# Third layer of a four-layer graph network: VectorE fills destination rows 40 columns ahead of the running sums instead of 48

## The chip, the core and the metric

The kernel runs on one core of one Trainium2 chip. The metric is the device time of the whole program in microseconds (us): the median of several executions. The rows shown come from one further execution, which the hardware profiler recorded.

## The reference

Four layers of message passing over one graph, each followed by a residual and a layer norm. The graph has 6250 nodes of 64 features and 106250 edges, sorted by destination. The third layer, the only one that the change touches, is an attention layer with six heads:

```python
def _L2_gnn_ref(x, edge_idx, W_l, W_r, att, bias):      # the third layer
    ...
    gl = (x @ W_l).reshape(n, H, F_OUT)                   # H = 6, F_OUT = 64
    gr = (x @ W_r).reshape(n, H, F_OUT)
    s = jax.nn.leaky_relu(gl[src] + gr[dst], NEG_SLOPE)
    e = jnp.einsum('ehf,hf->eh', s, att)                  # a logit for each edge and head
    m = jax.ops.segment_max(e, dst, num_segments=n)
    p = jnp.exp(e - m[dst])
    denom = jax.ops.segment_sum(p, dst, num_segments=n)
    alpha = p / (denom[dst] + 1e-16)
    msg = alpha[:, :, None] * gl[src]
    out = jax.ops.segment_sum(msg, dst, num_segments=n)
    out = out.mean(axis=1) + bias
    return jax.nn.selu(out)
...
x = _layernorm(x + _L0_gnn_ref(...)); x = _layernorm(x + _L1_gnn_ref(...))
x = _layernorm(x + _L2_gnn_ref(x, edge_index, ...));  x = _layernorm(x + _L3_gnn_ref(...))
```

## The kernel before

The edges stand as a table of 128 partitions by NC = 832 columns, so that a column holds 128 edges, one for each partition, and each partition walks through 832 edges in the order of their destinations. The third layer goes through the columns in NCH = 52 chunks of CH = 16. Five queues work on it, all written out by hand, with semaphores between them. Instructions of one queue start in the order in which they stand.

**GpSimd (POOL), `g2_chunk`.** One indirect DMA for each column gathers the 128 rows of the source nodes (table `xt2`, both halves of 64 values alike) into the tile XS, which holds NX = 6 chunks. A gather into a column that was used six chunks ago waits for the sums of that column. The issuing line is the helper L193. The landings of eight columns are counted together: a semaphore for each half chunk.

**VectorE (DVE).** It has four kinds of work for each chunk c.
- `fill2(c, j)`, L1355: the second half of a gathered row is to be the destination's row. Where the edge has the same destination as the edge of the column before, the row is copied from there (a predicated copy of 64 values); else the gathered one stays. So the fills of all 832 columns are one chain, and each half chunk waits for its gathers to land (j = 0 and j = 8).
- `soft2(c, 0..5)`, L1466 to L1480: running maxima of the logits over a chunk, in six small instructions.
- `px2` (L1514), the products of the source rows with the first four heads' weights, two columns at a time, and `carry2` (L1502).
- `step2(c, j)`, L1548 for j = 0 and L1550 for the rest: the running sum of 390 values over the columns. Here it is "the sum" of column j.

In the loop the order for each j is: a fill of a column further on, for j = 8, 9 and 10 two instructions of `soft2(c + 1)` around the sum, the sum, and after each even j a `px2`. The next chunk begins with `carry2`.

**TensorE (PE).** `chunk2_t(c)` takes a chunk in four quarters of four columns: `pt_t` transposes four columns (L1367), `pm_t` multiplies the quarter before by the weights in three pieces (L1382), and at the second quarter `pe_t` and `pf_t` (L1398, L1411) make the logits of chunk c - 1. Before quarters 0 and 2 it waits for the fill of column 7 and of column 15.

**ScalarE (ACT).** `exp2_a(c + 1)` (L1489, L1490, L1495) needs all of `soft2(c + 1)`. Behind it in the queue come 18 items of chunk c + 3 from A_ORDER, mixed with 33 items of `px2_a(c + 1)` (L1528, then L1533: the products for the last two heads, from which each pair of sums waits). Items 0, 4, 8 and 12 are the copies of the transposed quarters (`pt_a`, L1374), three items behind each are `pm_a` (L1389), and items 16 and 17, which stand behind item 7, copy the logits of chunk c + 2 (`pe_a` L1406, `pf_a` L1416):

```python
for n, i in enumerate(A_ORDER):      # 0..7, 16, 17, 8..15
    if c + 3 < NCH:
        chunk2_a(e, c + 3, i)
    ...
    while at * 18 < (n + 1) * 33:
        px2_a(e, c + 1, at)
        at += 1
```

The items of `px2_a` are numbered from 0 (L1528) to 32. Before the sum of an even column j the product item 2j + 4 must be done: item 4 for j = 0, item 16 for j = 6, item 20 for j = 8, item 32 for j = 14.

**SyncE** stores the sums of a chunk (3.2 MB) once its last sum is done.

Of the kernel before, what the change touches and what calls it, by code (L numbers as in the profile page):

```python
# [12 lines left out]
NC = 832  # L13
EP = P * NC
CH = 16
NCH = NC // CH
# [44 lines left out]
def gathered_before(L, b):  # L61

    late = sum(16 * CH // 2 for n in (N0, N1)[0:L] if b == (NCH - 1) % n)
    return sum(16 * CH // h * len(range(b // h, NCH, n)) for n, h in ((N0, 1), (N1, 1), (NX, 2), (4, 1))[0:L] if b // h < n) - late
# [8 lines left out]
def bc(a, shape):  # L76
    return a.broadcast_to(shape)
# [6 lines left out]
def build(nc, x, src, dst, et16, et8, w0, beta, wl, wr, att, bias2, w3, coeff, hbias, loopw, out):  # L84
# [22 lines left out]
    with ExitStack() as ctx:  # L107
# [12 lines left out]
        S = {n: ctx.enter_context(nc.semaphore("k_" + n)) for n in names}  # L120
# [1186 lines left out]
        def xsv(c):  # L1307
            return XS[:, c % NX, :].rearrange("p (j d) -> p j d", j=CH)
# [7 lines left out]
        def q2_at(c):  # L1316
            return 6 * c - 2 if c else 0

        def f2_at(c, j):

            if c < 4:
                return 16 * c + j + 1
            return 64 + 9 * (c - 4) + (9 if j == 15 else (j + 1) // 2 + (j == 14))

        def g2_chunk(e, c, general):
            for j in range(CH):
# [15 lines left out]
        def fill2(e, c, j):  # L1342
            cur, prv = xsv(c), xsv(c - 1)
            if j % 8 == 0:
                k = 2 * (c % NX) + j // 8
                e.wait_ge(S[f"g_{k}"], gathered_before(2, k) + 8 * CH * (c // NX + 1))
            if c == 0 and j == 0:
                e.wait_ge(S["xdi"], 32)
                v.tensor_copy(cur[:, 0, D:P], xi2[:, 0:D]).then_inc(S["f2"], 1)
                return  # L1350
            if c >= 4 and j % 2 and j < CH - 1:
                e.wait_ge(S["t2"], 16 * (c - 3) + j - 1)
            else:
                e.wait_ge(S["f2"], f2_at(c, j - 1) if j else f2_at(c - 1, CH - 1))
            m = v.copy_predicated(cur[:, j, D:P], bc(gi[:, c * CH + j:c * CH + j + 1], [P, D]),  # L1355
                                  cur[:, j - 1, D:P] if j else prv[:, CH - 1, D:P])
            if c < 4 or j % 2 or j == CH - 2:
                m.then_inc(S["f2"], 1)

        def pt_t(e, u):  # L1360
            c, q = divmod(u, NGR)
            if q % 2 == 0:
                e.wait_ge(S["f2"], f2_at(c, 4 * q + 7))
            if u >= 2:
                e.wait_ge(S["at"], u - 1)
            for i in range(4):
                m = t.transpose(PS[u % 2][:, i * P:(i + 1) * P], xsv(c)[:, 4 * q + i, :], ident[:])  # L1367
            m.then_inc(S["pt"], 1)
# [83 lines left out]
        def soft2(e, c, i):  # L1452

            Sp = s2v(c - 1)
            pq = pf2[:, c % 2, H * CH:H * CH + H]
            if c == 0 and i in (1, 5):
                return
            n = q2_at(c) + (i - 1 if c == 0 and i else i)
            if n:
                e.wait_ge(S["q2"], n)  # L1460
            if i == 0:
                e.wait_ge(S["ab"], c + 1)
                e.wait_ge(S["init"], 17)
                if c:
                    e.wait_ge(S["am"], c)
                m = v.tensor_copy(Bf[:, :, 1:CH], bc(Bn[:, c * CH + 1:(c + 1) * CH].unsqueeze(1), [P, H, CH - 1]))  # L1466
            elif i == 1:
                m = v.scalar_tensor_tensor(out=eb[:, :, 0], in0=Sp[:, CH - 1, HW:], scalar=Bn[:, c * CH:c * CH + 1],
                                           in1=eb[:, :, 0], op0=ALU.add, op1=ALU.max)
            elif i == 2:  # L1470
                m = v.tensor_tensor_scan(mf2.rearrange("p h j -> p (h j)"), Bf.rearrange("p h j -> p (h j)"),  # L1471
                                         eb.rearrange("p h j -> p (h j)"), -BIG, ALU.add, ALU.max)
            elif i == 3:
                m = v.tensor_tensor_scan(mb2.rearrange("p h j -> p (h j)")[:, ::-1], Bb[:, 1:][:, ::-1],  # L1474
                                         mf2.rearrange("p h j -> p (h j)")[:, ::-1], -BIG, ALU.add, ALU.max)
            elif i == 4:
                m = v.tensor_tensor(p2v(c).rearrange("p h (q i) -> p h q i", q=4), logits,
                                    mb2.rearrange("p h (q i) -> p h q i", q=4), ALU.subtract)
            else:
                m = v.scalar_tensor_tensor(out=pq, in0=Sp[:, CH - 1, HW:], scalar=Bn[:, c * CH:c * CH + 1],  # L1480
                                           in1=mb2[:, :, 0], op0=ALU.add, op1=ALU.subtract)
            m.then_inc(S["q2"], 1)
# [14 lines left out]
        def carry2(e, c):  # L1497

            pq = pw2[c % 2][:, H * CH:H * CH + H]
            e.wait_ge(S["ax"], c + 1)  # L1500
            e.wait_ge(S["t2"], 16 * c - 1)
            v.tensor_tensor(tmp2, s2v(c - 1)[:, CH - 1, 0:HW].rearrange("p (h d) -> p h d", h=H),  # L1502
                            bc(pq.unsqueeze(2), [P, H, 65]), ALU.mult)

        def px2(e, c, k):

            n = HV
            cols = slice(2 * k, 2 * k + 2)
            pe_ = pw2[c % 2][:, 0:H * CH].rearrange("p (h j) -> p j h", h=H)
            if k == 0:  # L1510
                e.wait_ge(S["ax"], c + 1)
                if c >= 2:
                    e.wait_ge(S[f"s_{c % 2}"], stored_before(2, c % 2) + 16 * (c // 2))
            m = v.tensor_tensor(s2v(c)[:, cols, 0:n * 65].rearrange("p j (h d) -> p j h d", h=n)[:, :, :, 0:D],  # L1514
                            bc(xsv(c)[:, cols, 0:D].unsqueeze(2), [P, 2, n, D]),
                            bc(pe_[:, cols, 0:n].unsqueeze(3), [P, 2, n, D]), ALU.mult)
            if k == 0:
                m.then_inc(S["p2"], 1)
# [18 lines left out]
        def step2(e, c, j):  # L1537
            if c == 0 and j == 0:
                return
            Sv = s2v(c)  # L1540
            if j == 0 or (c == 0 and j == 1):
                e.wait_ge(S["p2"], c + 1)
            if j % 2 == 0 or (c == 0 and j == 1):
                e.wait_ge(S["ap"], 8 * c + j // 2 + 1)
            if c or j > 1:
                e.wait_ge(S["t2"], 16 * c + j - 1)
            if j == 0:
                m = v.tensor_tensor(Sv[:, 0, 0:HW], Sv[:, 0, 0:HW], tmp2.rearrange("p h d -> p (h d)"), ALU.add)  # L1548
            else:
                m = v.scalar_tensor_tensor(out=Sv[:, j, 0:HW], in0=Sv[:, j - 1, 0:HW],  # L1550
                                           scalar=gf[:, c * CH + j:c * CH + j + 1], in1=Sv[:, j, 0:HW],
                                           op0=ALU.mult, op1=ALU.add)
            m.then_inc(S["t2"], 1)

        def layer2_v(e):
            vc.hold()
            v.memset(Bb, -BIG).then_inc(S["init"], 1)
            for c in range(2):
                for j in range(CH):
                    fill2(e, c, j)  # L1560
            for i in range(6):
                soft2(e, 0, i)
            for j in range(CH):
                fill2(e, 2, j)
            for c in range(NCH):
                if c:
                    carry2(e, c)
                px2(e, c, 0)
                for j in range(CH):
                    if c + 3 < NCH:  # L1570
                        fill2(e, c + 3, j)
                    if c + 1 < NCH and 8 <= j < 11:
                        soft2(e, c + 1, 2 * j - 16)
                    step2(e, c, j)
                    if c + 1 < NCH and 8 <= j < 11:
                        soft2(e, c + 1, 2 * j - 15)
                    if j % 2 == 0 and j + 2 < CH:
                        px2(e, c, j // 2 + 1)
                    if c == NCH - 1 and j < 13:
                        if j == 0:  # L1580
                            e.wait_ge(S["am"], NCH)
                        mend_max_v(e, vc, 2, T2, H, B2, j)
# [706 lines left out]
        def _(e):  # L2289
# [128 lines left out]
            with e.If(oneway2 != 0):  # L2418
                e.wait_ge(S["xt"], 64 * NG)
                exchange_v(e, 2)  # L2420
            layer2_v(e)
            mend_soft_v(e, vc, 2, T2, H, B2)
            e.wait_ge(S["fr"], 1)
# [135 lines left out]
```

## Time and profile before

| what | value |
|---|---|
| median of 3 runs | 4737.09 us (4735.63 to 4739.78) |
| profiled execution: time | 4745.29 us |
| profiled execution: span | 4743.1 us |
| third layer's column loop | from about 2335 to 3464 us of the span |
| busy over the whole span | POOL 72%, DVE 58%, ACT 35%, PE 31% |
| busy tenths in the slices of the loop | DVE 8, ACT 8, PE 8, POOL 7 |

The span runs from the first to the last instruction; the time of the profiled execution is 2.2 us longer, and 8.2 us above the median. In the rows below, a row of the timeline gives start, duration, engine, line and operation, how many instructions are merged, and in brackets how long the engine sat idle before it and what ended that. A row of the windows gives, for each engine, busy time and count of instructions, then TensorE's granted clock as a share of full speed, the DMA engines' busy share and GB/s.

### The profile page before, as it was taken

To read this page: it belongs to the slowest core of one execution; us is meant where nothing else is said; L and a number is where in the kernel's file an instruction comes from. 1 tells how busy PE (TensorE), PEld (TensorE's weight loads), DVE (VectorE), ACT (ScalarE), POOL (GpSimd) and SP (SyncE) were. 2 spreads that over 40 slices of the span, in tenths; PEclk is the share of its full clock that TensorE was granted. 3 is DMA by queue.
4 is the path that set the end of the run, shared out by engine and by line. 5 is a ranking of instruction groups with operands and counts; after the bars stand their busy time and mean duration, and the time that the engine had idled before them with its cause. 6 is when DMAs were issued, how large, how long until landed. Compare 5 with 4: busy or idle time off the path is not lost.

```text
span 4743.1 us, 28267 instructions
## 1 busy us (share of the span) xinstructions
PE 1448.4 (31%) x6129; PEld 722.0 (15%) x6129; DVE 2738.1 (58%) x5205; ACT 1643.2 (35%) x3774; POOL 3421.7 (72%) x3538
## 2 busy tenths in 40 slices
PE   7721111000000000001788888888832000000003
PEld 3610000000000000000333333333332000000002
DVE  4684443116555555556378888888875444444444
ACT  2232212220011111112378888888842222221121
POOL 6777777776777777776577777777454777777776
PEclk9955555555555555555899999999965555555555
DMA  7222222223233333332245555555541222222222
GB/s 279 51 75 52 50 50 53 53 55 56 71 80 80 80 80 80 80 81 73 50 161 216 204 201 216 214 197 209 198 140 48 79 80 79 79 72 78 79 79 75
DMA packets 183555, 502.21 MB, mean 106 GB/s; under 512 B 91670, under 2 KB 94044, under 8 KB 167112
## 3 DMA queue, kind: packets, MB, share of 16 engines
q0 software_dynamic: 114560, 181.19, 17.4%
q1 hardware_dynamic: 66584, 316.93, 17.4%
q10 hardware_dynamic: 2224, 2.13, 0.2%
q8 instruction: 53, 0.87, 0.1%
q14 instruction: 134, 1.10, 0.1%
HBM read 185.63 MB, written 314.17 MB: 105 GB/s over the span
## 4 chain that ended last, share of the span: by engine, by line
POOL 29%; issue 10%; DVE 6%; DMA 4%; PE 2%; ACT 1%; POOLq 0%; DVEq 0%; SPq 0%; ACTq 0%
POOL AR L193 29%; DMA AR<-xt,Si 3%; DVE AR L1550 2%; DVE AR L1514 1%; PE ps L1242 0%; PE ps L1398 0%; PE ps L1719 0%; PE ps L1382 0%; DVE AR L1355 0%; ACT AR L1389 0%; ACT AR L1533 0%; DVE AR L1474 0%; DVE AR L1471 0%; ACT AR L1707 0%; PE ps L1726 0%
## 5 line engine op out<-in xcount | busy, mean ns | idle before, releaser
L193 POOL DMA_INDIRECT AR<-xt,Si x2496 | 2399.5, 961 | 807.3 <-issue 732.4
L193 POOL DMA_INDIRECT AR<-y,R x752 | 721.1, 959 | 234.8 <-issue 227.6
L1382 PE MATMUL ps<-AR,WLR 128*128 128x512 f32 x1248 | 612.9, 614 | 94.4 <-ACT AR L1389 94.4
L1865 DVE TENSOR_TENSOR AR<-AR,ps 128x2048 f32<-128x2048 f32 (+1 forms) x53 | 186.7, 3522 | 561.4 <-DMA AR<-xt,Si 561.4
L1533 ACT ACTIVATE AR<-AR 128x64 f32<-128x64 f32 x1664 | 498.5, 349 | 0.0
L1550 DVE SCALAR_TENSOR_TENSOR AR<-AR,gf 128x390 f32<-128x390 f32 x780 | 482.7, 619 | 5.7 <-ACT AR L1533 3.2
L1824 ACT COPY AR<-AR 128x2048 f32<-128x2048 f32 (+1 forms) x53 | 189.1, 3568 | 837.4 <-DVE AR L1883 837.4
L1389 ACT ACTIVATE AR<-ps 128x512 f32<-128x512 f32 x624 | 370.8, 594 | 70.0 <-PE ps L1382 68.6
L890 DVE SCALAR_TENSOR_TENSOR AR<-ps,AR 128x1024 f32<-128x1024 f32 x52 | 102.6, 1973 | 439.8 <-DMA AR<-xt,Si 439.8
L1174 PE MATMUL ps<-AR,ones 128*128 128x384 f32 (+1 forms) x6 | 3.7, 758 | 1072.2 <-DVE AR L1125 1072.2
L946 ACT ACTIVATE ps<-AR 128x17 f32<-128x17 f32 (+1 forms) x52 | 9.8, 188 | 911.4 <-DVE AR L930 884.1
L543 DVE SCALAR_TENSOR_TENSOR AR<-AR,gf 128x64 f32<-128x64 f32 x48 | 15.8, 328 | 490.7 <-ACT AR L527 490.7
L1355 DVE COPY_PREDICATED AR<-gf,AR 128x64 f32<-128x64 int32 x831 | 187.8, 226 | 188.7 <-DMA AR<-xt,Si 187.3
L193 POOL DMA_INDIRECT AR<-s,endi x196 | 219.3, 1119 | 95.5 <-issue 66.1
L1514 DVE TENSOR_TENSOR AR<-AR,ps 128x512 f32<-128x512 f32 x416 | 282.7, 680 | 0.0
L1382 PEld LDWEIGHTS ps<-AR,WLR 128*128 128x128 f32 x1248 | 215.0, 192 | 350.6 <-issue 258.3
L1914 PE MATMUL ps<-LW,AR 128*128 128x64 f32 (+1 forms) x98 | 24.1, 428 | 773.8 <-ACT AR L1906 773.8
L527 ACT COPY AR<-AR 128x1024 f32<-128x1024 f32 (+1 forms) x48 | 90.6, 1888 | 440.0 <-DMA AR<-y,R 440.0
L1883 DVE TENSOR_TENSOR_SCAN AR<-ps,AR 128x512 f32<-128x512 f32 x208 | 241.6, 1200 | 0.0
L375 PE MATMUL ps<-AR 128*128 128x196 bf16 x416 | 77.4, 367 | 514.3 <-DVE AR L368 514.3
L1398 PE MATMUL ps<-AR,A 128*32 128x512 f32 x1248 | 206.2, 628 | 0.0
L1174 PEld LDWEIGHTS ps<-AR,ones 128*128 128x128 f32 x6 | 1.7, 320 | 1073.2 <-DVE AR L1125 1072.6
(345 smaller groups left out, 3496.0 us busy)
## 6 DMA issues: line engine op xcount, KB each, us to landing
s<-AR SPq DMA_DIRECT2D x51, 3168.0 KB
s<-AR SPq DMA_DIRECT2D x51, 1024.0 KB, 4.0
AR<-xt,Si POOLq DMA_INDIRECT x2496, 2.5
s<-AR SPq DMA_DIRECT2D x53, 512.0 KB, 2.7
s<-AR SPq DMA_DIRECT2D x51, 528.0 KB, 3.0
y<-AR SPq DMA_DIRECT2D x24, 1024.0 KB, 4.1
AR<-y,R POOLq DMA_INDIRECT x752, 2.4
xt<-X SPq DMA_DIRECT2D x21, 224.0 KB, 3.1
```

Source lines behind the costliest of these rows:

```text
L193: g.indirect_dma_start(out=o, out_offset=None, in_=table, in_offset=bass.IndirectOffsetOnAxis(ap=idx, axis=0)).then_inc(S[sem], 16)
L890: m = v.scalar_tensor_tensor(out=tx1(c), in0=bc(gx1(c)[:, 0:CH].unsqueeze(1), [P, D, CH]), scalar=0.5, in1=g1v(c)[:, :, 65:R1].rearrange(" ...
L1355: m = v.copy_predicated(cur[:, j, D:P], bc(gi[:, c * CH + j:c * CH + j + 1], [P, D]), cur[:, j - 1, D:P] if j else prv[:, CH - 1, D:P])
L1382: t.matmul(PS[2 + k % 3][:], WLR[:, ch * P:(ch + 1) * P], XT2[:, u % 6, :], start=True, stop=True).then_inc(S["pm"], 1)
L1389: s.activation(RL2[:, u % 5, ch * 512:(ch + 1) * 512], PS[2 + k % 3][:], ACT.Relu).then_inc(S["ar"], 1)
L1398: m = t.matmul(PS[6][32 * q:32 * q + 32, :], w_, m_, start=(ch == 0), stop=(ch == 3))
L1514: m = v.tensor_tensor(s2v(c)[:, cols, 0:n * 65].rearrange("p j (h d) -> p j h d", h=n)[:, :, :, 0:D], bc(xsv(c)[:, cols, 0:D].unsqueeze(2) ...
L1533: m = s.activation(Sv[:, j, h * 65:h * 65 + D], xsv(c)[:, j, 0:D], ACT.Copy, scale=pe_[:, h, j:j + 1])
L1550: m = v.scalar_tensor_tensor(out=Sv[:, j, 0:HW], in0=Sv[:, j - 1, 0:HW], scalar=gf[:, c * CH + j:c * CH + j + 1], in1=Sv[:, j, 0:HW], op0= ...
L1824: s.copy(s3v(c)[:, j0:j0 + n, :], sum3(i).rearrange("p x j -> p j x")).then_inc(S["co"], 1)
L1865: v.tensor_tensor(sum3(i).rearrange("p (b d) j -> p j b d", b=NBS), bc(rows.unsqueeze(2), [P, n, NBS, D]), bc(CW3[:, i % 2, :, 0:n].rearra ...
L1883: v.tensor_tensor_scan(part, gx3(i)[:], part, 0.0, ALU.mult, ALU.add).then_inc(S["sc"], 1)
```

## The change

The number of columns that VectorE's fills run ahead of its sums becomes a constant, AHEAD = 40. Before, 48 columns (three chunks) were filled ahead of the loop, and at column j of chunk c the fill was that of column j of chunk c + 3. Now 40 are filled ahead, and at column 16c + j the fill is that of column 16c + j + 40: for j = 0 to 7 columns 8 to 15 of chunk c + 2, for j = 8 to 15 columns 0 to 7 of chunk c + 3. The semaphore counts follow.

```diff
+        AHEAD = 40
+
         def f2_at(c, j):
 
-            if c < 4:
-                return 16 * c + j + 1
-            return 64 + 9 * (c - 4) + (9 if j == 15 else (j + 1) // 2 + (j == 14))
+            at = CH * c + j
+            if at < AHEAD + CH:
+                return at + 1
+            k, i = divmod(at - AHEAD - CH, CH)
+            return AHEAD + CH + 9 * k + (9 if i == CH - 1 else (i + 1) // 2 + (i == CH - 2))
...
-            if c >= 4 and j % 2 and j < CH - 1:
-                e.wait_ge(S["t2"], 16 * (c - 3) + j - 1)
+            at = CH * c + j - AHEAD
+            if at >= CH and j % 2 and at % CH < CH - 1:
+                e.wait_ge(S["t2"], at - 1)
             else:
                 e.wait_ge(S["f2"], f2_at(c, j - 1) if j else f2_at(c - 1, CH - 1))
...
-            if c < 4 or j % 2 or j == CH - 2:
+            if at < CH or j % 2 or at % CH == CH - 2:
                 m.then_inc(S["f2"], 1)
...
-            for j in range(CH):
+            for j in range(AHEAD - 2 * CH):
                 fill2(e, 2, j)
...
                 for j in range(CH):
-                    if c + 3 < NCH:
-                        fill2(e, c + 3, j)
+                    if CH * c + j + AHEAD < NC:
+                        fill2(e, *divmod(CH * c + j + AHEAD, CH))
```

On VectorE's queue this is seen at the two ends of the layer; between them every fill has the same place among the sums and is one of a column eight earlier. Where the loop begins, the queue has before (L1355 is the fill, L1514 `px2`, L1550 the sum):

```order
L1471 SCALAR_TENSOR_TENSOR AR<-AR 128x96
L1474 SCALAR_TENSOR_TENSOR AR<-AR 128x96
L1477 TENSOR_TENSOR AR<-ps,AR 128x96
L1355 COPY_PREDICATED AR<-gf,AR 128x64 x16
L1514 TENSOR_TENSOR AR<-AR,ps 128x2x4x64
L1355 COPY_PREDICATED AR<-gf,AR 128x64
```

and in the change, whose lines are five further on (L1360 is the fill, L1519 `px2`):

```order
L1476 SCALAR_TENSOR_TENSOR AR<-AR 128x96
L1479 SCALAR_TENSOR_TENSOR AR<-AR 128x96
L1482 TENSOR_TENSOR AR<-ps,AR 128x96
L1360 COPY_PREDICATED AR<-gf,AR 128x64 x8
L1519 TENSOR_TENSOR AR<-AR,ps 128x2x4x64
L1360 COPY_PREDICATED AR<-gf,AR 128x64
```

Eight fills fewer stand ahead of the first `px2`. At the other end, the last fill before is that at column 15 of chunk 48, right ahead of the next chunk's `carry2` (L1502):

```order
L1355 COPY_PREDICATED AR<-gf,AR 128x64
L1550 SCALAR_TENSOR_TENSOR AR<-AR,gf 128x390
L1355 COPY_PREDICATED AR<-gf,AR 128x64
L1550 SCALAR_TENSOR_TENSOR AR<-AR,gf 128x390
L1502 TENSOR_TENSOR ps<-AR,ps 128x390
```

and in the change it is that at column 7 of chunk 49, right ahead of the first instruction of `soft2` (L1471):

```order
L1519 TENSOR_TENSOR AR<-AR,ps 128x2x4x64
L1360 COPY_PREDICATED AR<-gf,AR 128x64
L1555 SCALAR_TENSOR_TENSOR AR<-AR,gf 128x390
L1471 COPY AR<-Bn 128x6x15
L1555 SCALAR_TENSOR_TENSOR AR<-AR,gf 128x390
```

The eight fills have moved behind the first half of chunk 49. The order on TensorE, ScalarE, GpSimd and SyncE does not change.

## Rows read from the trace of the kernel before

**Rows 1.** Busy time by engine, TensorE's clock and DMA from loop start to the last gather.
```profile
2383.00:3394.00 1011.00, 878.50 (x3678) 350.13 (x3667) 850.49 (x2280) 831.29 (x2607) 772.99 (x782) 0.98 0.56 205
```

**Rows 2.** Waits, 2335 to 3450 us: engine, line, releaser: total, times, longest.
```profile
DVE AR L1355 <- DMA AR<-xt,Si: 187.3, 58, 8.0
...
ACT ps L1489 <- DVE AR L1480: 76.3, 43, 12.3
```

**Rows 3.** Timeline of POOL: the layer's last gather.
```profile
3393.68 0.96 POOL L193 DMA_INDIRECT AR<-xt,Si  x1 [0.30 <-issue]
```

**Rows 4.** Timeline of VectorE in chunks 28 and 29.
```profile
2983.34 0.23 DVE L1355 COPY_PREDICATED AR<-gf,AR 128x64 f32<-128x64 int32 x1 [2.74 <-DMA AR<-xt,Si]
...
2983.64 0.62 DVE L1550 SCALAR_TENSOR_TENSOR AR<-AR,gf 128x390 f32<-128x390 f32 x1
...
2991.05 0.23 DVE L1355 COPY_PREDICATED AR<-gf,AR 128x64 f32<-128x64 int32 x1
...
2993.12 0.55 DVE L1548 TENSOR_TENSOR AR<-AR,ps 128x390 f32<-128x390 f32 x1
...
2999.04 0.63 DVE L1550 SCALAR_TENSOR_TENSOR AR<-AR,gf 128x390 f32<-128x390 f32 x1
...
3000.18 0.23 DVE L1355 COPY_PREDICATED AR<-gf,AR 128x64 f32<-128x64 int32 x1
```

**Rows 5.** Timeline of ScalarE in the same chunks.
```profile
2978.87 0.57 ACT L1374 COPY AR<-ps 128x512 f32<-128x512 f32 x1
2979.34 0.59 ACT L1533 ACTIVATE AR<-AR 128x64 f32<-128x64 f32 x2
...
2985.79 0.37 ACT L1533 ACTIVATE AR<-AR 128x64 f32<-128x64 f32 x1
2987.18 0.26 ACT L1489 ACTIVATE ps<-AR 128x102 f32<-128x102 f32 x1 [1.01 <-DVE AR L1480]
...
2987.71 0.61 ACT L1374 COPY AR<-ps 128x512 f32<-128x512 f32 x1
...
2990.07 0.58 ACT L1533 ACTIVATE AR<-AR 128x64 f32<-128x64 f32 x2
...
2997.26 0.59 ACT L1406 COPY AR<-ps 128x512 f32<-128x512 f32 x1 [0.81 <-PE ps L1398]
2997.74 0.59 ACT L1533 ACTIVATE AR<-AR 128x64 f32<-128x64 f32 x2
```

**Rows 6.** Timeline of VectorE where the layer starts.
```profile
2341.56 2.10 DVE L1355 COPY_PREDICATED AR<-gf,AR 128x64 f32<-128x64 int32 x8 [4.72 <-DMA AR<-xt,Si]
...
2391.75 0.23 DVE L1355 COPY_PREDICATED AR<-gf,AR 128x64 f32<-128x64 int32 x1 [7.32 <-DMA AR<-xt,Si]
```

**Rows 7.** Timeline of TensorE where the layer starts.
```profile
2343.71 0.66 PE L1367 MATMUL ps<-ident,AR 128*128 128x128 f32 x4 [1.60 <-DVE AR L1355]
...
2347.22 2.74 PE L1382 MATMUL ps<-AR,WLR 128*128 128x512 f32 x6
...
2358.80 1.02 PE L1382 MATMUL ps<-AR,WLR 128*128 128x512 f32 x2
```

**Rows 8.** Timeline of ScalarE where the layer starts.
```profile
2344.41 0.59 ACT L1374 COPY AR<-ps 128x512 f32<-128x512 f32 x1 [1.66 <-PE ps L1367]
...
2365.85 0.59 ACT L1406 COPY AR<-ps 128x512 f32<-128x512 f32 x1 [1.29 <-PE ps L1398]
```

**Rows 9.** Timeline of VectorE at the end of the layer.
```profile
3406.18 0.22 DVE L1355 COPY_PREDICATED AR<-gf,AR 128x64 f32<-128x64 int32 x1
...
3424.50 0.57 DVE L1502 TENSOR_TENSOR ps<-AR,ps 128x390 f32<-128x390 f32 x1 [0.41 <-ACT AR L1490]
```

**Rows 10.** Timeline of TensorE: pauses of over 3 us.
```profile
2471.36 1.10 PE L1382 MATMUL ps<-AR,WLR 128*128 128x512 f32 x2 [3.27 <-ACT AR L1389]
...
2637.96 2.05 PE L1382 MATMUL ps<-AR,WLR 128*128 128x512 f32 x2 [3.34 <-ACT AR L1389]
```

**Rows 11.** A window of 2 us right behind the second of these pauses.
```profile
2638.00:2640.00 2.00, 2.00 (x6) 0.50 (x10) 2.00 (x7) 2.00 (x8) 1.39 (x3) 0.50 0.13 33
```

## The prediction

> **What bounds the kernel now.** I read the windows first, to see which engine is short of work in the third layer's loop. [rows 1] says none is the plain bound: in 1011 us VectorE is busy 84%, ScalarE 82%, TensorE 87%. GpSimd issues 782 gathers there, one each 1.293 us, which is 20.7 us for the 16 of a chunk. Then the waits. VectorE's only large one is a fill that waits for gathers, 187.3 us in 58 waits; ScalarE waits 76.3 us for the last instruction of `soft2` [rows 2]. The last gather of the layer still waits for nothing but its issue [rows 3], so GpSimd has never been held by a full buffer: its 20.7 us a chunk set the pace, and VectorE waits for it once a chunk, 2.74 us at column 8 of chunk 28 [rows 4]. What VectorE itself needs is then about 18 us a chunk. The chain through ScalarE is to be seen in the timeline. In chunk 29 the products for the sum of column 6 (item 16) end at 2997.74 + 0.59 = 2998.33 [rows 5] and the sum starts at 2999.04 [rows 4]. It has 0.7 us to spare. So two bounds lie close together: gathers at 20.7 us, and a ring from VectorE's fill through TensorE and ScalarE back to VectorE's sums.
>
> **What the change does to the gathers.** It adds no instruction and takes none away. A fill needs its gather eight sums later than before, which is ten more microseconds of slack; but a stream that is paced by its issue does not go faster for it. Were the gathers still the bound, the gain would come once: at the last landing only 40 columns of sums would be left instead of 48.
>
> **What it does to the ring.** ScalarE's copy of the first quarter of chunk c + 3 (item 0) stands right behind the exponentials of chunk c + 1 and ahead of all their products. It needs the fill of column 7 of chunk c + 3. That fill stood at column 7 of chunk c; it now stands at column 15. Before, ScalarE reached the copy at 2987.71 [rows 5], long after the fill. Now the fill comes at 2991.05 [rows 4], after ScalarE is ready. So the ring closes, and I walk once round it, with F = 0 at the start of the fill at column 15 of chunk c and no clock change:
>
> 1. Fill to copy. Where TensorE waited for a fill at the start, the fill's group ends at 2343.66 [rows 6], the transposes start at 2343.71 [rows 7], the copy at 2344.41 [rows 8]: 0.05 + 0.70. With the fill's own 0.23 the copy starts at 0.98.
> 2. First sum of chunk c + 1: item 4 of the products is the first of the pair at 2990.07, 2.36 after the copy, and one takes about 0.35 [rows 5], so the sum can start at 3.7. VectorE alone would be there at 2.07 (2993.12 - 2991.05 [rows 4]). A wait of 1.6.
> 3. TensorE: from the first transposes to the products of the second quarter 3.51 (2347.22 - 2343.71 [rows 7]), to ScalarE's copy of the logits 7.05 (2358.80 [rows 7] to 2365.85 [rows 8]). From 0.28 that is 10.84. Items 15 and 16 stand behind that copy and end 1.07 after its start (2997.26 to 2997.74 + 0.59 [rows 5]): 11.9. The sum of column 6 cannot start before. This is the tightest place: from the first sum's 3.7 VectorE would take 5.9 to it (2999.04 - 2993.12 [rows 4]) and be there at 9.6. It is held by 2.3 us.
> 4. The fill at column 7 of chunk c + 1 comes 1.14 later (3000.18 - 2999.04 [rows 4]): 13.1. It is now the fill of column 15 of chunk c + 3, for which TensorE's third quarter waits. The same 0.98: ScalarE's copy of the third quarter at 14.1. Items 19 and 20 end 1.06 after such a copy (2978.87 to 2979.34 + 0.59 [rows 5]): the sum of column 8 at 15.15, where VectorE alone would have been there 1.1 earlier.
> 5. From the sum of column 8 to the fill at column 15: 7.41 (2991.05 - 2983.64 [rows 4]). The round ends at 22.56.
> 6. Does ScalarE allow it? From the third quarter's copy to the end of item 32 it takes 7.29 (2978.87 to 2985.79 + 0.37 [rows 5]): 21.35, then 0.53 for the exponentials (2987.71 - 2987.18 [rows 5]), ready at 21.9; the next copy is due at 22.56 + 0.98. Yes, with 1.6 us over.
>
> So a round takes **22.6 us** where the gathers need 20.7, and GpSimd runs ahead until the six buffered chunks hold it.
>
> **The sum.** The fill at column 15 of chunk 0 comes 7.7 us (2991.05 - 2983.34 [rows 4]) after the gathers of chunk 3's first half land at 2391.75 [rows 6]: 2399.5. From there 48 rounds to the same place in chunk 48, which is 3406.2 before [rows 9]. With 22.56: 2399.5 + 1082.9 = 3482.4, so 76 us later. Chunk 49 is one more such round, about 23.4 to the next `carry2` against 18.3 before (3424.50 - 3406.18 [rows 9]): 5 more. Chunks 50 and 51 have no fills in either and cost the same. The start, eight columns earlier, is in the sum already. Without a change of clock: **+81 us**.
>
> **TensorE's clock.** In step 4 TensorE has done all it can about 3.0 us before the next fill: its last three pieces start 3.51 after the third quarter's transposes (13.4) and take 2.74 [rows 7], to 19.6, and the next transposes start at 22.8. A pause of 3.2 us in each round. In this trace five pauses of 3.1 to 3.6 us stand in the loop. After one, of 3.27 us, two matmuls took 1.10; after the other four the clock was low, as after that of 3.34 us, where they took 2.05 [rows 10] and the granted clock was 0.50 [rows 11], the 1.2 GHz level. Of the fourteen pauses of 2.2 to 2.9 us four were followed by a low clock. From the 2 us windows each low stretch lasted 3.4 us, one 6.8. At half the clock 3.4 us cost 1.7 us of TensorE's work, and now that work lies on the ring (steps 1 and 3). I take three rounds in four (the five pauses say four in five, the shorter ones less): 0.75 x 1.7 = 1.3, a round of 23.85 us and 48 x 1.3 = 62 more. The sum is 81 + 62 = **+143 us**. The bounds are 0 (never low) and 48 x 1.7 = 82 (always low).
>
> The Trainium skill (TensorE: Matmul & The Clock Gate, "What's actually happening") says that the throttled clock is the default and activity lifts it, in two states. The trace agrees: 0.50 or 1.00. [...]
>
> Against the profiled execution's 4745.3 that gives 4888. It ran 8 us above the median of the three runs, 4737.1, so I forecast **4880 us**.
>
> **The rivals.**
> - *The clock stays up*: the ring as walked, +81: 4737 + 81 = 4818. For it: the pause of 3.27 us, and ten of the fourteen pauses of 2.2 to 2.9 us. Against it: the four other long ones. Chance 0.20.
> - *Low in every round*, some for 6.8 us: a round of 24.3 or more, +81 + 82 = +163 and up, 4900 to 4935. For it: a ring repeats itself, so that each pause may meet the same fate. Chance 0.12.
> - *The ring is shorter than walked* and ends within about 0.9 us of the gathers' 20.7: +5 to +45, 4742 to 4782. The walk adds delays seen at the start of the layer, under another load. Against it: the 0.7 us that the sum of column 6 has to spare is less than any of its terms. Chance 0.07.
> - *The gathers stay the bound*, the other side: it decides if the round is under 20.7 us, so my walk would have to be 1.9 us too long. The steady state stays as it is, and the end comes eight sums earlier, about 1.1 us each (17.5 us a chunk without fills, from the 18.3 of [rows 9]): -9, 4728. For it: VectorE's 2.74 us wait in each chunk, which takes up that much of any delay. Chance 0.05.
> - *The change does not do what it says*: the queue shows eight fills fewer ahead of the loop and the last one in chunk 49, so I give this no chance.
>
> **How the numbers follow.** The forecast has 0.56, its own range 4845 to 4910 (half or all rounds low, and 0.3 us either way in the round). Leaving out the two cheap rivals (0.12) and the far end of the dear one, the range is 4790 to 4930. Measurements of this kernel tell 0.2%, 9 us, from no change. Faster: most of the fourth rival, 0.04. Same: 0.02. Slower: 0.94.
>
> **What would show it.** Right: in the loop VectorE no longer waits for gathers but for ScalarE's products, at columns 0, 6 and 8; the copy behind the exponentials waits for TensorE and TensorE for the fill; `carry2` comes every 22.6 us, or near 24 where the granted clock dips; GpSimd waits for sums or products late in the layer. Step 3 is wrong if the sum of column 6 does not wait. Wrong altogether: `carry2` every 20.7 us and fills that still wait for gathers. The other stages must not move. The weakest number is how often the clock falls: it alone moves the sum by 82 us.

## The result and the profile after

| | median | runs |
|---|---|---|
| before | 4737.55 us | 4735.63 to 4739.78, 4 runs |
| changed | 4896.54 us | 4891.77 to 4898.83, 4 runs |

The ratio is 1.0336, with the interval 1.0323 to 1.0349: 159 us slower. The forecast was 4880, the range 4790 to 4930. The profiled execution took 4894.83 us, 149.5 more than that of before. Its page has these lines; PEclk is TensorE's clock in tenths, a slice is 122 us:

```profile
span 4893.1 us, 28267 instructions
...
PEclk9855555555555555558899999999966555555555
...
L1555 DVE SCALAR_TENSOR_TENSOR AR<-AR,gf 128x390 f32<-128x390 f32 x780 | 483.6, 620 | 170.4 <-ACT AR L1538 169.1
...
L1372 PE MATMUL ps<-ident,AR 128*128 128x128 f32 x832 | 154.5, 317 | 230.9 <-DVE AR L1360 230.9
L1360 DVE COPY_PREDICATED AR<-gf,AR 128x64 f32<-128x64 int32 x831 | 187.7, 226 | 32.1 <-DMA AR<-xt,Si 30.9
```

The windows from the loop's start to its end, in the columns of [rows 1]:

```profile
2378.00:3542.00 1164.00, 913.11 (x3670) 375.34 (x3668) 853.23 (x2272) 846.26 (x2601) 765.62 (x783) 0.92 0.48 179
```

The same work takes 1164 us instead of 1011 with every engine less busy, VectorE 73% instead of 84%, and TensorE's mean clock fell from 0.98 to 0.92. No engine became the bound; a ring of waits did. The waits of the layer (engine, line, releaser: total, times, longest):

```profile
PE ps L1372 <- DVE AR L1360: 225.0, 101, 3.8
...
DVE AR L1555 <- ACT AR L1538: 169.1, 153, 1.9
ACT AR L1379 <- PE ps L1372: 162.4, 102, 4.3
DVE AR L1553 <- issue: 140.1, 48, 3.6
...
POOL AR L193 <- ACT AR L1538: 88.4, 92, 3.0
POOL AR L193 <- DVE AR L1555: 76.2, 121, 1.7
...
DVE AR L1360 <- DMA AR<-xt,Si: 30.9, 7, 8.0
...
ACT ps L1494 <- DVE AR L1485: 3.7, 1, 3.7
```

Against [rows 2], the fills' wait for gathers has gone from 187.3 us to 30.9, ScalarE's for `soft2` from 76.3 to 3.7. In their place TensorE waits for the fill, ScalarE for TensorE's transposes, VectorE for ScalarE's products, and GpSimd is held by full buffers. The first sum (L1553) waits 2.9 us each time and the view calls it "issue"; by the timelines below, what ends just before it is product item 4 on ScalarE.

One round on VectorE (start, duration, engine, line):

```profile
2706.98 0.23 DVE L1360 COPY_PREDICATED AR<-gf,AR 128x64 f32<-128x64 int32 x1
...
2712.00 0.56 DVE L1553 TENSOR_TENSOR AR<-AR,ps 128x390 f32<-128x390 f32 x1 [2.86 <-issue]
...
2720.23 0.62 DVE L1555 SCALAR_TENSOR_TENSOR AR<-AR,gf 128x390 f32<-128x390 f32 x1 [1.90 <-ACT AR L1538]
...
2721.37 0.23 DVE L1360 COPY_PREDICATED AR<-gf,AR 128x64 f32<-128x64 int32 x1
...
2723.45 0.62 DVE L1555 SCALAR_TENSOR_TENSOR AR<-AR,gf 128x390 f32<-128x390 f32 x1 [1.07 <-ACT AR L1538]
...
2730.87 0.23 DVE L1360 COPY_PREDICATED AR<-gf,AR 128x64 f32<-128x64 int32 x1
```

On ScalarE:

```profile
2708.41 0.58 ACT L1379 COPY AR<-ps 128x512 f32<-128x512 f32 x1 [2.02 <-PE ps L1372]
...
2711.56 0.58 ACT L1538 ACTIVATE AR<-AR 128x64 f32<-128x64 f32 x2
...
2719.13 0.59 ACT L1411 COPY AR<-ps 128x512 f32<-128x512 f32 x1 [0.81 <-PE ps L1403]
...
2722.34 0.59 ACT L1379 COPY AR<-ps 128x512 f32<-128x512 f32 x1 [1.16 <-PE ps L1372]
```

On TensorE:

```profile
2707.26 1.12 PE L1372 MATMUL ps<-ident,AR 128*128 128x128 f32 x4 [3.25 <-DVE AR L1360]
2708.17 3.64 PE L1387 MATMUL ps<-AR,WLR 128*128 128x512 f32 x6
2711.64 0.60 PE L1372 MATMUL ps<-ident,AR 128*128 128x128 f32 x4
...
2721.65 0.66 PE L1372 MATMUL ps<-ident,AR 128*128 128x128 f32 x4 [1.23 <-DVE AR L1360]
2722.14 2.74 PE L1387 MATMUL ps<-AR,WLR 128*128 128x512 f32 x6
...
2731.15 1.12 PE L1372 MATMUL ps<-ident,AR 128*128 128x128 f32 x4 [3.25 <-DVE AR L1360]
```

The round is 23.89 us (2730.87 - 2706.98). Counted from the start of the fill at column 15, the walk of the prediction against the trace (us):

| place | walk | trace | late by |
|---|---|---|---|
| copy of the first quarter | 0.98 | 1.43 | 0.45 |
| first sum | 3.7 | 5.02 | 1.3 |
| copy of the logits | 10.84 | 12.15 | 1.31 |
| sum of column 6 | 11.9 | 13.25 | 1.3 |
| fill at column 7 | 13.1 | 14.39 | 1.3 |
| sum of column 8 | 15.15 | 16.47 | 1.3 |
| next round | 22.56 | 23.89 | 1.33 |

All of the lateness arises in TensorE's first two rows. The four transposes are followed by the next work after 0.91 us, where in the third quarter of the same round it is 0.49; the six products after 3.47 instead of 2.58. That is 0.42 + 0.89 = 1.31 us, and nothing is added after it. The first sum, at 2712.00, waits for the first of the two product items merged in the row at 2711.56. The granted clock (last but two of each row) at that place, one round earlier, in windows of 2 us:

```profile
2682.00:2684.00 2.00, 0.64 (x3) 0.64 (x4) 1.90 (x6) 0.49 (x3) 1.68 (x2) 0.67 0.23 66
2684.00:2686.00 2.00, 2.00 (x6) 0.97 (x5) 1.25 (x3) 1.00 (x3) 1.41 (x2) 0.50 0.73 286
2686.00:2688.00 2.00, 2.00 (x8) 0.99 (x7) 0.00 (x0) 1.78 (x6) 1.42 (x2) 0.98 1.12 482
```

Reckoned from full clock to half, the low stretch is (0.33 + 0.50 + 0.02) / 0.5 x 2 = 3.4 us, the same as in before. But it begins about 0.7 us before TensorE resumes (2 us less the 0.64 busy is 1.36 idle, and 1.32 us of this window are low), so only some 2.7 us of it lie on work and cost half of that.

### The profile page after: what moved, and what is told of

It is laid out like the page before. It is cut to its first block, busy times and chain, and to the rows that moved or that the text cites. A ratio compares the mean times of both kernels' runs of the same rounds, so it can differ in the third digit from the quotient of the medians.

```text
span 4893.1 us, 28267 instructions
## 1 busy us (share of the span) xinstructions
PE 1489.5 (30%) x6129; PEld 753.0 (15%) x6129; DVE 2742.9 (56%) x5205; ACT 1659.6 (34%) x3774; POOL 3410.4 (70%) x3538
## 4 chain that ended last, share of the span: by engine, by line
POOL 19%; PE 14%; DVE 11%; issue 8%; ACT 2%; DMA 1%; DVEq 0%; SPq 0%; ACTq 0%; POOLq 0%
POOL AR L193 19%; PE ps L1387 7%; DVE AR L1555 5%; PE ps L1403 4%; DVE AR L1519 3%; PE ps L1372 2%; ACT AR L1538 1%; DVE AR L1360 1%; ACT AR L1411 1%; PE ps L1242 0%; DVE AR L1479 0%; DVE AR L1476 0%; DMA AR<-s,endi 0%; DMA s<-AR 0%; DVE AR L1485 0%
## 5 line engine op out<-in xcount | busy, mean ns | idle before, releaser
L1387 PE MATMUL ps<-AR,WLR 128*128 128x512 f32 x1248 | 659.6, 656 | 0.0
L1519 DVE TENSOR_TENSOR AR<-AR,ps 128x512 f32<-128x512 f32 x416 | 283.0, 680 | 1.7 <-ACT AR L1495 1.7
L1387 PEld LDWEIGHTS ps<-AR,WLR 128*128 128x128 f32 x1248 | 240.8, 214 | 272.6 <-issue 221.4
L1372 PE MATMUL ps<-ident,AR 128*128 128x128 f32 x832 | 154.5, 317 | 230.9 <-DVE AR L1360 230.9
L1360 DVE COPY_PREDICATED AR<-gf,AR 128x64 f32<-128x64 int32 x831 | 187.7, 226 | 32.1 <-DMA AR<-xt,Si 30.9
L1379 ACT COPY AR<-ps 128x512 f32<-128x512 f32 x208 | 120.9, 581 | 168.2 <-PE ps L1372 168.2
```

What stands on the lines that cost most here:

```text
L1387: t.matmul(PS[2 + k % 3][:], WLR[:, ch * P:(ch + 1) * P], XT2[:, u % 6, :], start=True, stop=True).then_inc(S["pm"], 1)
```

## The experiments

Each kernel is the changed one with the edit shown. Where a number of a round is given, it is the distance of one `carry2` (L1507 in the change) from the next.

### The pause filled: warm40

```diff
 # end of chunk2_t, once a chunk
+            for _ in range(4):
+                t.matmul(PS[0][:, 0:3 * P], ident[:], WLR[:, 0:3 * P], start=True, stop=True)
```

> The change (40 ahead) with four matmuls of 384 columns more at the end of each chunk on TensorE, written to a free PSUM bank that nobody reads, about 2.6 us in its pause of 3.25 us. Theory (ring plus clock): the granted clock stays near 1.00, the copy of the first quarter comes 0.98 us after the fill instead of 1.43, a round takes 22.6 us instead of 23.9, the kernel about 4820 us. Rival (the pause is only a sign that TensorE has nothing to do, and the round is set elsewhere): the clock rises and the round stays 23.9 us, about 4897 us.

Measured: 4878.97 us, 1.0295 (1.0279 to 1.0310). Only 18 us came back, not the 77 of the theory. TensorE's timeline:

```profile
2702.74 2.74 PE L1438 MATMUL ps<-WLR,ident 128*128 128x384 f32 x8
2705.85 0.66 PE L1372 MATMUL ps<-ident,AR 128*128 128x128 f32 x4 [0.37 <-DVE AR L1360]
...
2718.93 1.12 PE L1372 MATMUL ps<-ident,AR 128*128 128x128 f32 x4 [1.23 <-DVE AR L1360]
2719.84 3.95 PE L1387 MATMUL ps<-AR,WLR 128*128 128x512 f32 x6
```

Two windows of 24 us, with the clock as the last but two:

```profile
2454.00:2478.00 24.00, 21.80 (x89) 9.19 (x92) 17.85 (x48) 17.78 (x55) 18.21 (x20) 0.93 0.53 190
2494.00:2518.00 24.00, 21.39 (x89) 9.10 (x88) 18.66 (x50) 18.86 (x59) 18.15 (x20) 1.00 0.57 205
```

The pause of 3.25 us is down to 0.37, and after it the transposes take 0.66: full clock. The clock falls instead at the pause of 1.23 us before the third quarter, which the extra matmuls do not reach. In 11 of the 48 rounds the clock stayed at 1.00, and these take 22.57 or 22.58 us; the others take 23.9 to 24.0. So the walk's 22.56 is confirmed, and so is the cost of one fall. That the clock depends on the long pause alone is refuted, and so is the rival: where the clock stays up, the round does get shorter.

### The tightest place relieved: items40

```diff
-                    while at * 18 < (n + 1) * 33:
+                    while at * 18 < (n + 1) * 33 or (n == 7 and at < 17):
```

Items 15 and 16 of the products then stand ahead of ScalarE's copy of the logits; the sum of column 6 waits for item 16.

> The change with items 15 and 16 of ScalarE's products ahead of its copy of the logits instead of behind it; ScalarE idles there for 0.8 us, so the copy is not delayed. Theory (the sum of column 6, which needs item 16, is the tightest place of the ring): that sum starts about 1.3 us earlier, the sum of column 8 then waits for the copy of the third quarter, and a round loses 1.3 us: 22.6 with a low clock in each round, about 4835 us. Rival (the wait of the first sum, the longest one seen, sets the round): no change, about 4897 us.

Measured: 4822.88 us, 1.0177 (1.0162 to 1.0193). The rounds take 21.3 us where the clock stays up, in 19 of 48, and 22.8 to 24.0 where it falls; the expectation had 22.6 in each. The place of two items on ScalarE was worth 74 us, the clock's part in it included: step 3 holds the ring.

### Both: both40

The two edits together.

> Both edits together. Theory: they touch different terms and add: 22.57 - 1.3 = 21.3 us a round, 0.6 above the pace of the gathers, about 4765 us. Rival (the two share one slack): no better than the better of the two alone, about 4820 us.

Measured: 4767.31 us, 1.0059 (1.0044 to 1.0075). The window of [rows 1], here:

```profile
2383.00:3394.00 1011.00, 935.40 (x3962) 400.25 (x3961) 835.21 (x2223) 815.75 (x2549) 740.69 (x780) 1.00 0.56 202
```

The clock is 1.00 in every round but the first, and the rounds behind that one (23.00) are 21.3 us, against a mean of 20.76 before (2410.66 to 3407.03 in 48 rounds). The 48 rounds together take 28 us more than before (2397.97 to 3422.39), chunk 49 takes 6 more (23.5 against 17.5), and the start gives 10 back (the first `carry2` comes 65.5 us behind the first fill, 75.7 before): 24 us, where the medians differ by 27.5. VectorE's wait for gathers from 2400 to 3390 is 2.0 us, against 143.9 before: a ring, only a shorter one, is still the bound. The place of the items and the clock together are worth 129 us of the loss (4896.5 - 4767.3); the rest is the shorter ring.

### A lead of 44: a44

```diff
-        AHEAD = 40
+        AHEAD = 44
```

> The change with 44 columns ahead instead of 40, so that the fill for which ScalarE's first copy waits stands at column 11. Theory: the ring without waits is then 17.9 us from fill to fill, 19.2 with a low clock, under the 20.7 us of the gathers; the gathers pace the loop as before the change, and only the end comes four sums earlier: 4733 us, ratio 0.999. Rival (each column less of lead costs its share): half of the loss, about 4817 us.

Measured: 4751.01 us (11 runs), 1.0023 (1.0013 to 1.0032): 18 us above the forecast. The loss of 159 us is down to 11, yet the kernel is not faster. Two waits of VectorE, one `carry2` between them:

```profile
2833.15 0.24 DVE L1360 COPY_PREDICATED AR<-gf,AR 128x64 f32<-128x64 int32 x1 [3.62 <-DMA AR<-xt,Si]
...
2845.61 0.57 DVE L1507 TENSOR_TENSOR ps<-AR,ps 128x390 f32<-128x390 f32 x1
...
2854.25 0.23 DVE L1360 COPY_PREDICATED AR<-gf,AR 128x64 f32<-128x64 int32 x1 [2.86 <-DMA AR<-xt,Si]
```

VectorE waits for gathers again, 148.6 us in the loop, so the ring is not the bound in most rounds. But the round is 21.1 us, not 20.76: the gathers themselves have become slower. GpSimd's timeline in a stretch between the two:

```profile
2836.30 0.94 POOL L193 DMA_INDIRECT AR<-xt,Si  x1 [0.30 <-issue]
2837.55 1.23 POOL L193 DMA_INDIRECT AR<-xt,Si  x1 [0.30 <-issue]
2839.08 1.55 POOL L193 DMA_INDIRECT AR<-xt,Si  x1 [0.30 <-issue]
2840.94 0.94 POOL L193 DMA_INDIRECT AR<-xt,Si  x1 [0.30 <-issue]
```

And VectorE's, the copy and the two scans of `soft2`:

```profile
2837.23 0.20 DVE L1471 COPY AR<-Bn 128x90 f32<-128x90 f32 x1
...
2838.75 0.35 DVE L1476 TENSOR_TENSOR_SCAN AR<-AR 128x96 f32<-128x96 f32 x1
...
2839.54 0.34 DVE L1479 TENSOR_TENSOR_SCAN AR<-AR 128x96 f32<-128x96 f32 x1
```

The two gathers issued while `soft2` runs take 1.23 and 1.55 us instead of 0.94. In the next chunk one (2860.18) takes 1.55 again.

### Stores in halves: a44half, a44half_2, b48half, b48half_2

The landings in a44 took up to 9.3 us from their issue, 4.4 before, so a rival was that a fill waits behind the 3.2 MB store. Each store is cut in two, with the lead at 44 and, as a control, at 48 (the semaphore counts that follow are not shown):

```diff
-                n = CH // 4 if c == NCH - 1 else CH
+                n = CH // 4 if c == NCH - 1 else CH // 2
```

> 44 ahead, and each chunk's sums stored in two halves, the first as soon as the sum of column 7 is done (the semaphore counts follow). The run with 44 had most rounds at 21.1 us. Theory (the store closes a ring): a store of 3.2 MB keeps the DMA queues full for 8.3 us from the end of a chunk, gathers that are issued then land at its end, and with 44 ahead the fill that waits for them stands at column 4, 12.5 us ahead of the next chunk's end: 8.6 + 12.5 = 21.1. Half stores take half as long, so the ring opens and the gathers' own pace of about 20.7 us is back: about 4733 us. Rival (the low clock in TensorE's pauses lengthens the rounds of 44): no change, about 4751 us.

> Control: 48 ahead as before the change, with the stores in halves. Theory (the store matters only where a fill waits for it early in a chunk): with 48 the fill that waits stands at column 8, 11.8 us behind the store's start, so at most a few us: 4733 to 4740 us. Rival (halved stores help the gathers of any version): 15 us or more, under 4723 us.

The first runs of these two and of the next pair fell on a chip where the kernel before itself took 5480.96 us. There a44half took 5476.91 us (0.9993, 0.9981 to 1.0006) and b48half 5475.88 (0.9989, 0.9974 to 1.0004). The rounds of a44half took 24.7 us there on average, so they say nothing of what makes 21.1 out of 20.7 elsewhere. Both ran again on another chip:

> 44 ahead with each chunk's sums stored in two halves, once more, on a chip where the kernel before takes its usual 4740 us. Theory (the store closes a ring with 44 ahead: 8.6 us from its start to the landing that the fill at column 4 waits for, 12.5 to the next chunk's end): rounds back from 21.1 to about 20.6 us, 4733 us. Rival (the low clock in TensorE's pauses makes the 21.1): about 4751 us as with 44 alone.

> Control: 48 ahead with the stores in halves, on such a chip. Theory (landings behind a store matter only where a fill waits for them early in a chunk): 4733 to 4740 us. Rival (halved stores speed up the gathers of any version): under 4723 us.

Measured: a44half_2 4748.08 us, 1.0014 (1.0005 to 1.0023); b48half_2 4742.27, 1.0005 (0.9996 to 1.0014). Halving the stores gives back 3 us of 18, if anything: the rival's time, not the theory's 4733. The store alone is not the cause.

### A lead of 42 with all three edits: a42items, a42all, a42all_2

a42items has AHEAD = 42 and the item's place; a42all the extra matmuls and the halved stores too.

> 42 ahead, with items 15 and 16 ahead of the copy of the logits. The decisive fill stands at column 13. Ring without waits: 13.9 from that fill to the sum of column 8, 6.0 from there to the next such fill, 19.9 us, and up to 1.7 more with a low clock, 21.6. Against the gathers' 20.7 it is a mixture, about 20.9 us: 4745 us. Rival (what counts is only that the fill comes before ScalarE is ready for its copy, which at column 13 it does not): a loss like that with 40 and this edit in part, 4790 us.

> 42 ahead, items 15 and 16 first, the stores in halves, and the four extra matmuls a chunk that keep TensorE's clock up. Theory: with the three rings all under the gathers' pace, nothing is left of the change but its end, six sums of 1.1 us earlier: 4731 us. Rival (some ring not yet seen): 4745 us or more.

On the chip named above: 5514.86 us (1.0062, 1.0039 to 1.0086) and 5555.41 (1.0133, 1.0105 to 1.0161), losses of 34 and 74 us against the kernel before there; why they are so large on that chip is open. The second ran again on the other chip:

> 42 ahead, items 15 and 16 first, stores in halves, four extra matmuls a chunk, on such a chip. Theory: all rings are under the gathers' pace (the ring through ScalarE is 19.9 us, with the clock up), so only the end is left, six sums of 1.1 us earlier: 4731 us, rounds of about 20.6 us with fills that wait for gathers. Rival (a ring not yet seen): 4745 us or more.

Measured: 4755.59 us, 1.0030 (1.0018 to 1.0042). The theory's 4731 is missed by 25 us. The clock is 1.00, the ring is relieved, the store is halved, VectorE waits for gathers in both halves of a chunk (161.0 us), and still a round is 21.08 us. Between two gathers GpSimd is idle for 0.3 us, whatever ends it, and never longer, so nothing holds it back either. What is left is the gathers' own time on GpSimd. a42items was not run again, so its 4745 stands untested.

### A lead of 56: a56

```diff
-        AHEAD = 40
+        AHEAD = 56
...
-            for j in range(AHEAD - 2 * CH):
-                fill2(e, 2, j)
+            for j in range(AHEAD - 2 * CH):
+                fill2(e, *divmod(2 * CH + j, CH))
```

> The other way: 56 columns ahead, eight more than before the change. Theory (the gathers pace the loop, lead costs only at its end): the same rounds as with 48, and eight sums more behind the last landing, 8 x 1.1 = 9 us: 4748 us. Rival (the ring through ScalarE counts in the loop of before too, so that more lead helps): faster than before, 4720 us or less.

Measured: 4748.31 us, 1.0015 (1.0006 to 1.0024), with rounds of 20.64 us. While gathers pace the loop, eight columns more of lead cost 7 us, once (the first `carry2` comes 85.4 us behind the first fill, 75.7 before).

The gathers of these kernels in one window, 2400 to 3380 us, POOL being the last of the five busy times. The kernel before:

```profile
2400.00:3380.00 980.00, 857.57 (x3578) 341.19 (x3578) 827.97 (x2223) 809.87 (x2538) 749.28 (x758) 0.98 0.57 207
```

a56:

```profile
2400.00:3380.00 980.00, 850.84 (x3548) 337.19 (x3549) 831.30 (x2224) 804.68 (x2522) 748.97 (x759) 0.97 0.56 207
```

a44:

```profile
2400.00:3380.00 980.00, 846.41 (x3544) 341.28 (x3543) 808.38 (x2179) 806.17 (x2506) 752.35 (x748) 0.96 0.57 206
```

a42all_2:

```profile
2400.00:3380.00 980.00, 919.12 (x3922) 394.74 (x3921) 814.09 (x2184) 804.54 (x2513) 753.26 (x745) 1.00 0.57 205
```

both40:

```profile
2400.00:3380.00 980.00, 910.37 (x3863) 389.39 (x3862) 811.39 (x2160) 794.11 (x2482) 727.65 (x767) 1.00 0.57 204
```

One gather takes 0.988 us before, 0.987 with 56, 1.006 with 44, 1.011 with 42 and 0.949 in both40, where VectorE hardly waits for them. Between 0.988 and 1.006 lie 16 x 0.0174 = 0.28 us a chunk, 13 us over 48 rounds: most of a44's missing 18.

Where a gather falls against `soft2` decides how long it takes, in the kernel before as well. Two of its chunks, each with the start of the second scan (L1474):

```profile
2612.43 0.34 DVE L1474 TENSOR_TENSOR_SCAN AR<-AR 128x96 f32<-128x96 f32 x1
2612.58 0.94 POOL L193 DMA_INDIRECT AR<-xt,Si  x1 [0.30 <-DVE AR L1550]
...
2695.12 1.55 POOL L193 DMA_INDIRECT AR<-xt,Si  x1 [0.31 <-issue]
...
2695.57 0.35 DVE L1474 TENSOR_TENSOR_SCAN AR<-AR 128x96 f32<-128x96 f32 x1
```

Both gathers end 1.1 us behind the start of that scan, as does a44's at 2839.08 (2839.54 to 2840.63). The same holds, within 0.02 us, for 346 of the 352 gathers in this window that start at most 0.47 us ahead of that scan or 0.17 behind it, in eight traces (before, the change, a44, a56, both40, a44half_2, a42all_2, b48half_2). Every gather of 1.5 us or more in this window, 9 before, 10 in a56, 38 in a44, 42 in a42all_2 and none in both40, has the second scan start 0.42 to 0.46 us behind its own start.

## Why the forecast was right, and where it was not

- **The gathers**: right. With VectorE no longer waiting for them GpSimd is held by full buffers, and the last gather is issued at 3480.84, 87 us later than [rows 3].
- **The ring, steps 1 to 6**: right in every place, and in the sum to 0.01 us. 22.56 walked, 22.57 measured where the clock stays up, column 6 the tightest (items40).
- **The start and the end.** The first `carry2` comes at 2395.96, 14.7 us earlier than before (2410.66), as the walk had it: 48 rounds counted from 2399.5, 4.5 less because the layer itself began that much earlier (first fill 2330.5 against 2335.0). From the last such fill to the next `carry2` chunk 49 took 24.84 us (3553.14 to 3577.98) where 23.4 was forecast, and chunk 50 took 17.02, as before (17.03).
- **The clock term**: the product held, its factors did not, and that they made up for each other was luck. Forecast was three rounds in four by 1.7 us, 1.3 a round. The clock was low in every round, and cost 1.31: the 3.4 us stretch began while TensorE was still idle. The second rival had the frequency right, and put a price on it that no ordinary round paid; the measured 4896.5 lies just under its 4900. The count of the shorter pauses in before was one low: behind the pause of 2.74 us that ends at 2408.11 the clock is 0.54 from 2408 to 2410, so it was five of fourteen.
- **What was missing**: three rounds of 27.0 us, 3.1 more each. In the one from 3021.87 to 3048.89 the low stretch at the first quarter is twice as long (the six products take 5.33 us, not 3.64) and the clock falls once more at the pause of 1.23 us. 48 rounds took 1158.04 us (2395.96 to 3554.00), 24.13 each; 0.28 over the forecast's 23.85 is 13 us, 9 of it in these three. Why the clock stays low for longer in them is open.
- **From the trace to the median**: taking off the 8 us was right. From the first fill to the end of the last sum the layer takes 1127.7 us before (2335.0 to 3462.7) and 1285.7 in the change (2330.5 to 3616.2). That is 158 us more, and the medians differ by 159. The profiled execution of before was 8 us slower outside the layer, 4.5 ahead of it and 3.5 behind it, so the two profiled executions differ by 149.5 only. Against 158 the sum of +143 is 15 short: 13 in the 48 rounds and 1.4 in chunk 49.
- **The rival of no loss** failed at once in the chain: no fill waits for a gather in the steady state. a44 is the case that it described, with 4 us to gain for four columns, and even there no gain is to be seen: the slower gathers cost 13.

**The slower gathers of a44: seen in every trace, isolated by no run.** The ring, the clock and the store are each taken away in a42all_2 and the slow rounds stay. The gathers that overlap an instruction of `soft2` take 34 us beyond 0.945 us each in a44 and 13 before; the other gathers 12 and 21. Those of 1.5 us or more stand at one place against the second scan in all traces, and in a44 VectorE's rhythm, set by the landings, brings one there in 38 chunks, before in only 9. That VectorE's work makes them long is argued from this; no run moved `soft2` alone, or measured a gather beside these instructions alone. The Trainium skill (SBUF — State Buffer, "SBUF: two separate sides", and its box on the "DVE blocks DMA" trap) says that VectorE and GpSimd share a pair of ports, which one instruction holds whole, and that some VectorE copies so keep GpSimd from writing a DMA's descriptors. The rows agree in kind; which instruction holds the pair here, if one does, is open.

A lead below 39 was not tried: by the order of the queues the fill of column 7 of chunk c + 3 would stand behind a sum whose products stand behind ScalarE's copy of that same quarter, and the program would stop.

## What to carry to other kernels

How far one engine works ahead of itself is a wait for all engines that read its result. Before shortening a lead, walk from that result through the other queues back to the engine, counting what stands in front in each queue; if the walk is longer than the present period, it is the new period, whatever the busy shares say. And add TensorE's clock to such a walk: here, with a pause of 3.25 us in each round, the fall came back in every one.

## What the runs showed of the hardware

- The granted clock fell at the pause of 3.25 us in every round, while in the kernel before it had once stayed up through one of 3.27 us [rows 10]. With the long pause filled it fell at that of 1.23 us in most rounds, with TensorE busy in 21.80 of 24 us.
- A low stretch of 3.4 us costs half of only that part of it in which TensorE works: 1.31 us here, and 1.7 where it lies wholly on work, as the second half of the long ones does (5.33 - 3.64).
- The indirect gather of 128 rows takes 0.94 us of GpSimd, but single ones up to 1.56 beside small copies and scans of VectorE, and by their place: the gather beside the second scan ends 1.1 us behind that scan's start. In both40, where the scan starts 0.1 us ahead of the gather, it takes 0.99 us. 16 gathers took 15.2 us in both40 and 16.2 in a42all_2.
